# A Perceiver layer on one core: projections in halves, and copies batch by batch

## The chip, the core and the metric

The kernel runs on one core of a Trainium2 chip. The core has five engines with an instruction stream each: PE (matrix products; its weight loads are listed as PEld), DVE (element-wise vector work), ACT (functions and copies with a scale or bias), POOL (general element-wise work) and SP (here it only issues DMA transfers). The engines wait for each other through semaphores. SBUF is the on-chip memory, 128 partitions wide; PE writes its results into the eight banks of PSUM. The metric is the device time of one launch in microseconds, the median of several runs; lower is better.

## The reference

The kernel computes one layer on x of shape 2 x 256 x 512 (two batches of 256 tokens): cross-attention to a context of 2 x 4096 x 256, causal self-attention, and a mixture of experts, each on a normalised input (less its mean, over the root of its variance plus 1e-5) and added to x.

```python
# self-attention, 16 heads of 32 columns:
Q = proj_split(q_w, q_b)
K = proj_split(k_w, k_b)
V = proj_split(v_w, v_b)
S = jnp.einsum('hid,hjd->hij', K, Q) * SCALE
decay = jnp.where(delta < 0, 0.0, -delta.astype(jnp.float32) ** ALPHA)
S = jnp.where(delta < 0, -jnp.inf, S) + decay
C = jax.nn.softmax(S, axis=-1)
attn = jnp.einsum('hij,hjd->hid', C, V)
...
return attn @ o_w.T + o_b
# experts: a gate picks two of 8 per token (not shown), and a shared one:
sh = gelu(xt @ sw1 + sb1) @ sw2 + sb2
sh = sh + gelu(xt @ swd) @ swu
out = out + 0.2 * sh
# the layer:
x = x + _L0_xattn_ref(_layernorm(x, axis=-1), ctx_1024, mask_BxS2_bf1, ...)
x = x + _L0_attn_ref(_layernorm(x, axis=-1), ...)
x = x + _L0_ffn_ref(_layernorm(x, axis=-1), ...)
```

## The kernel before

Four stages follow one another: `queries` (to about 50 us), `cross` (to about 1419), `selfattn` (1420 to 1531) and `experts` (1532 to the end). Many products are made in three parts: an operand is split into a rounded high half (names in `h` or `_hi`, written by ACT) and the rest (`l` or `_lo`, written by DVE), and high x low, low x high and high x high are summed in PSUM. A product over 512 input columns so takes 3 x 4 = 12 matrix instructions of 128 rows each. The order of the work on each engine is the order in which the code is written; nothing reorders it.

**Cross-attention.** A unit is one key-value head of one batch. Its 4096 context tokens come in 8 stretches `n` of 4 steps `q`. At each step ACT copies the turned probabilities (`pth`, L688), DVE makes the rest (`ptl`, L860), and PE multiplies with the values (L1096). In the first part of batch 1 (`first_part(1)`) ACT also makes the high halves of that batch's value weights (`values_weight_high`, L742, twice, at n = 2 and n = 6) and of the output weight (`output_weight_high`, L716, at n = 2), and DVE the rest (`values_weight_low`, L915). All three stand at the head of their stretch, before its step q = 0.

**Self-attention.** `xn`, the normalised input, is turned on PE and split (`xh`, `xl`, L1376). Values for both batches, query 0 and key 0 are projected (`project`, L1447; 12 products of 128 x 512). Then come N = 8 units: unit n is chunk n // 2 of four heads, for batch n % 2. A unit has two turns `it` (query rows of the first and of the second 128 tokens). For a unit: PE makes all scores (L1474, sixteen records), DVE adds the mask and takes the maximum (L1318), ACT the exponential (L1394), DVE the reciprocal of the sum (L1326), POOL the scaling (L1270; of the second turn DVE does half, L1330), PE turns the probabilities (L1492), ACT and DVE copy them (`cT`, L1399, L1343), PE multiplies with the values (L1504), and ACT and DVE store the output's halves (L1403, L1334). The units overlap: in body n PE first issues the scores of unit n + 1, then the first turn of unit n, then the values of unit n - 1, then the second turn of unit n. Queries and keys of the chunks 1 to 3 are made beside the units, as tables say: `QUERY_BESIDE = {0: 1, 1: 2, 3: 3}` and `KEY_BESIDE = {0: 1, 2: 2, 4: 3}`. A query is copied out of PSUM by DVE (`query`, L1292), a key by ACT (`key`, L1380); both use one bank, `made`, so each projection waits until the one before has been copied. The scores of a chunk wait for its query and key.

**Experts' front.** `xn` of the third normalisation is turned on PE batch by batch (L2011). ACT copies the turned input twice, 512 columns (both batches) at a time: rounded (`xTh`, L1904) and whole (`xnT`, L1905); DVE makes the rest `xTl` from PSUM (L1766). ACT's root of the variance of batch 1 (`ln_root`, L107) stands before these copies. PE then makes the gate's logits (L2018, eight records) from `xnT`, and the shared expert's first product (L2027). The rest of the stage, to the end, is PE's work on the shared expert and the eight experts.

`WARM` is a number of priming products of the identity at the head of a stage, before PE's first wait.

## Time and profile before

| | us |
|---|---|
| median of 3 runs | 1980.34 |
| lowest and highest | 1979.60, 1981.26 |
| the profiled execution's own time | 1978.39 |
| its span in the profile | 1976.7 |
| mean granted clock of PE (1 is the full 2.4 GHz) | 0.987 |
| PE busy | 1909.9 (97%) |
| DVE busy | 1095.7 (55%) |
| ACT busy | 979.2 (50%) |
| POOL busy | 328.9 (17%) |

The profiled execution is 1.95 us under the median, and its own time is 1.69 us more than its span. Busy shares are averages over four stages. The lines of a timeline give start, duration, engine, source line, operation, output and inputs, and a count where equal instructions follow one another; in brackets stand the idle time before and what ended it. The durations of such a group include the tail of the last instruction, so starts are compared with starts. The windows split the span into stretches and give each engine's busy time with the count of its instructions.

### The profile page before, as it was taken

To read this page: it belongs to the slowest core of one execution; us is meant where nothing else is said; L and a number is where in the kernel's file an instruction comes from. 1 tells how busy PE (TensorE), PEld (TensorE's weight loads), DVE (VectorE), ACT (ScalarE), POOL (GpSimd) and SP (SyncE) were. 2 spreads that over 40 slices of the span, in tenths; PEclk is the share of its full clock that TensorE was granted. 3 is DMA by queue.
4 is the path that set the end of the run, shared out by engine and by line. 5 is a ranking of instruction groups with operands and counts; after the bars stand their busy time and mean duration, and the time that the engine had idled before them with its cause. 6 is when DMAs were issued, how large, how long until landed. Compare 5 with 4: busy or idle time off the path is not lost. (4 is left out here: it accounts for less than half of the span.)

```text
span 1976.7 us, 32080 instructions
## 1 busy us (share of the span) xinstructions
PE 1909.9 (97%) x10486; PEld 1602.1 (81%) x10486; DVE 1095.7 (55%) x2443; ACT 979.2 (50%) x2075; POOL 328.9 (17%) x238
## 2 busy tenths in 40 slices
PE   9999999999999999999999999999877899999998
PEld 6787888888888778878888888887655688999997
DVE  3667677677667666776677676676645531000002
ACT  3204676576577572065775776676544442122111
POOL 0300211211211213011211212211642300000001
PEclk9999999999999999999999999999988999999999
DMA  8651111111111146501111111111300907577552
GB/s 245 211 195 44 41 43 40 50 32 50 45 32 37 43 155 199 169 25 46 33 51 40 37 45 40 37 43 55 105 1 1 353 18 265 196 269 263 203 187 66
DMA packets 123281, 198.12 MB, mean 100 GB/s; under 512 B 12741, under 2 KB 62021, under 8 KB 119104
## 3 DMA queue, kind: packets, MB, share of 16 engines
q1 hardware_dynamic: 119040, 188.59, 28.6%
q10 hardware_dynamic: 2880, 4.55, 0.7%
q0 software_dynamic: 1280, 3.93, 0.6%
q8 instruction: 47, 0.77, 0.2%
q14 instruction: 34, 0.28, 0.0%
HBM read 151.50 MB, written 45.81 MB: 100 GB/s over the span
## 5 line engine op out<-in xcount | busy, mean ns | idle before, releaser
L860 DVE TENSOR_TENSOR crs_ptl<-crs_tp,crs_pth 128x512 fp32r<-128x512 f32 x512 | 352.7, 690 | 178.9 <-ACT crs_pth L688 178.3
L688 ACT ACTIVATE crs_pth<-crs_tp 128x512 fp32r<-128x512 f32 x504 | 301.6, 599 | 245.1 <-PE crs_tp L1086 241.9
L606 POOL TENSOR_TENSOR crs_vl<-crs_vraw,crs_vh 128x512 fp32r<-128x512 f32 x128 | 164.9, 1288 | 1071.2 <-ACT crs_vh L695 1071.1
L1077 PE MATMUL crs_ring<-crs_kh,crs_ql 128*128 128x512 f32 x512 | 233.9, 457 | 0.3 <-DVE crs_kl L864 0.3
L1096 PE MATMUL crs_ov<-crs_ptl,crs_vh 128*128 128x512 f32 x512 | 209.8, 410 | 9.6 <-DVE crs_ptl L860 7.7
L1096 PE MATMUL crs_ov<-crs_pth,crs_vh 128*128 128x512 f32 x512 | 202.5, 396 | 0.0
L1077 PE MATMUL crs_ring<-crs_kh,crs_qh 128*128 128x512 f32 x512 | 202.2, 395 | 0.0
L1077 PE MATMUL crs_ring<-crs_kl,crs_qh 128*128 128x512 f32 x512 | 201.3, 393 | 0.0
L1096 PE MATMUL crs_ov<-crs_pth,crs_vl 128*128 128x512 f32 x512 | 199.6, 390 | 0.0
L1086 PEld LDWEIGHTS crs_tp<-all_ident,crs_prob 128*128 128x128 f32 x1024 | 143.3, 141 | 69.1 <-ACT crs_more L677 4.2
L1086 PE MATMUL crs_tp<-all_ident,crs_prob 128*128 128x128 f32 x1024 | 195.3, 272 | 3.3 <-ACT crs_more L677 3.3
L677 ACT ACTIVATE crs_prob<-crs_prob,crs_nmax 128x512 f32<-128x512 f32 (+1 forms) x192 | 166.5, 868 | 63.3 <-DVE crs_nmax L875 63.3
L1086 PE MATMUL crs_tp<-all_ident,crs_more 128*128 128x128 f32 x1024 | 195.9, 273 | 0.0
L870 DVE CUSTOM_DVE_ANT_0 crs_more<-crs_ring,crs_maskb 128x512 f32<-128x512 f32 x256 | 172.7, 682 | 0.0
L870 DVE CUSTOM_DVE_ANT_0 crs_prob<-crs_ring,crs_maskb 128x512 f32<-128x512 f32 x256 | 172.5, 682 | 0.2 <-DVE attn_norm_ln_rstd L119 0.2
L677 ACT ACTIVATE crs_more<-crs_more,crs_nmax 128x512 f32<-128x512 f32 (+1 forms) x192 | 166.1, 865 | 0.0
L1878 DVE TENSOR_SCALAR ex_yT<-moe_bank,moe_b_cols 128x160 f32<-128x160 f32 x32 | 10.8, 379 | 273.1 <-PE moe_bank L2150 273.1
L864 DVE TENSOR_TENSOR crs_kl<-crs_ring,crs_kh 128x512 fp32r<-128x512 f32 x128 | 88.4, 691 | 132.0 <-ACT crs_kh L699 132.0
L1965 ACT ACTIVATE ex_hT<-moe_bank,moe_b_cols 128x160 f32<-128x160 f32 x128 | 43.5, 391 | 235.4 <-PE moe_bank L2126 235.4
L2126 PE MATMUL moe_bank<-moe_bufT,moe_w 128*128 128x160 f32 x1024 | 145.2, 302 | 0.7 <-ACT moe_bufT L1960 0.7
L2126 PEld LDWEIGHTS moe_bank<-moe_bufT,moe_w 128*128 128x128 f32 x1024 | 141.3, 192 | 2.8 <-ACT ex_hT L1965 1.0
L1086 PEld LDWEIGHTS crs_tp<-all_ident,crs_more 128*128 128x128 f32 x1024 | 127.9, 141 | 0.0
(283 smaller groups left out, 3344.0 us busy)
## 6 DMA issues: line engine op xcount, KB each, us to landing
moe_w<-in_L_ffn_w SPq DMA_DIRECT2D x48, 1024.0 KB, 12.7
v_scratch<-crs_more SPq DMA_DIRECT2D x64, 512.0 KB, 2.9
crs_vraw<-v_scratch SPq DMA_DIRECT2D x128, 256.0 KB, 2.7
ex_w<-in_L_ffn_w SPq DMA_DIRECT2D x16, 1024.0 KB, 13.9
crs_prob<-in_ctx SPq DMA_DIRECT2D x16, 512.0 KB, 4.7
crs_wo<-in_L_xattn_Wo SPq DMA_DIRECT2D x16, 512.0 KB, 4.2
moe_w<-in_L_ffn_sw SPq DMA_DIRECT2D x8, 1024.0 KB, 13.4
qry_wq<-in_L_xattn_Wq SPq DMA_DIRECT2D x16, 256.0 KB, 3.6
```

Of the source, the lines that this page charges most:

```text
L606: nc.gpsimd.tensor_tensor(vl[:, n % VR, :, :], vraw[:, :, :], vh[:, n % VR, :, :].bitcast(F32), ALU.subtract).then_inc(s["v_lo"], 1)
L677: act.activation(w, w, ACT.Exp, bias=nmax[:, t:t + 1], accum_out=rs[:, t, PIECE_OF[n]:PIECE_OF[n] + 1]).then_inc(s["p_ready"], 1)
L688: act.activation(pth[:, k % PT, :], tp[k % PT][:, :], ACT.Copy).then_inc(s["pt_hi"], 1)
L860: v.tensor_tensor(ptl[:, k % PT, :], tp[k % PT][:, :], pth[:, k % PT, :].bitcast(F32), ALU.subtract).then_inc(s["pt_lo"], 1)
L864: v.tensor_tensor(kl[:, n % KR, :], ring[k_at(n, op) % RING][:, :], kh[:, n % KR, :].bitcast(F32), ALU.subtract).then_inc(s["ring_free"], 1)
L870: v.tensor_tensor_reduce(probs(t, n * BANK, (n + 1) * BANK), ring[at % RING][:, :], maskb[:, n * BANK:(n + 1) * BANK], op0=ALU.add, op1=AL ...
L1077: m = pe.matmul(ring[at % RING][:, :], a[:, t // RT, rows], w[:, n % KR, :], start=i == 0, stop=i == 2)
L1086: m = pe.transpose(tp[k % PT][:, t * P:(t + 1) * P], probs(t, k * P, (k + 1) * P), ident[:, :])
L1096: m = pe.matmul(ov[:, :], a[:, k // NC % VR, k % NC, :], w[:, k % PT, :], start=k == 0 and i == 0, stop=k == SCH - 1 and i == 2)
L1878: m = v.tensor_scalar(yT[:, c, :], y_ps[c // 2][:, c % 2 * SL:(c % 2 + 1) * SL], b_cols[:, bass.ds(e * KC + c, 1)], None, ALU.add)
L1965: m = act.activation(hT[:, 2 * n + q, :], h_ps[n % 2][:, q * SL:(q + 1) * SL], ACT.Gelu, bias=b1_cols[:, bass.ds(e * FC + (2 * n + q), 1)])
L2126: m = pe.matmul(h_ps[n % 2][:, q * SL:(q + 1) * SL], w1[i][:, c, fc * P:(fc + 1) * P], bufT[:, i, c, :], start=c == 0, stop=c == KC - 1)
```

## The change

**A, cross-attention.** In `first_part(1)` the value weights' copies move behind the first step of their stretch, and the output weight's copy behind the third, on ACT; DVE's rest of the value weights moves likewise. Batch 0 keeps its places.

```diff
@@ -750,13 +750,14 @@
                             exp_piece(u, 0, t)
                         exp_piece(u, 1, 0)
                         exp_piece(u, 1, 1)
-                    if n == (2 if b else 0):
-                        values_weight_high(b, 0)
-                    if b and n == 2:
-                        output_weight_high(u, first_base(b) + QT)
-                    if n == (6 if b else 3):
-                        values_weight_high(b, 1)
                     for q in range(NC):
+                        if q == (1 if b else 0):
+                            if n == (2 if b else 0):
+                                values_weight_high(b, 0)
+                            if n == (6 if b else 3):
+                                values_weight_high(b, 1)
+                        if b and n == 2 and q == 3:
+                            output_weight_high(u, first_base(b) + QT)
                         if b and n < SB:
                             pt_high(u, n * NC + q)
                             exp_ahead(u, n, q)
```

On ACT, at the start of stretch n = 2 of batch 1's first part, before (`crs_pth` are the probabilities' copies, `crs_kh` receives the value weights, `crs_woh` the output weight):

```order
L695 ACTIVATE crs_vh<-crs_vraw 128x512 [waits crs_pv_done,crs_v_ld]
L742 ACTIVATE crs_kh<-crs_more 128x1024 [waits crs_ring_full,crs_wv_ld]
L716 ACTIVATE crs_woh<-crs_wo 128x1024 [waits crs_ring_full,crs_wo_ld]
L688 ACTIVATE crs_pth<-crs_tp 128x512 [waits crs_pv_done,crs_pt_full]
L677 ACTIVATE crs_more,crs_rs<-crs_more,crs_nmax 128x1024 [waits crs_inv_chain,crs_max_ready]
L688 ACTIVATE crs_pth<-crs_tp 128x512 [waits crs_pv_done,crs_pt_full]
```

and now:

```order
L695 ACTIVATE crs_vh<-crs_vraw 128x512 [waits crs_pv_done,crs_v_ld]
L688 ACTIVATE crs_pth<-crs_tp 128x512 [waits crs_pv_done,crs_pt_full]
L677 ACTIVATE crs_more,crs_rs<-crs_more,crs_nmax 128x1024 [waits crs_inv_chain,crs_max_ready]
L742 ACTIVATE crs_kh<-crs_more 128x1024 [waits crs_ring_full,crs_wv_ld]
L688 ACTIVATE crs_pth<-crs_tp 128x512 [waits crs_pv_done,crs_pt_full]
L677 ACTIVATE crs_more,crs_rs<-crs_more,crs_nmax 128x1024 [waits crs_inv_chain,crs_max_ready]
L732 ACTIVATE all_w_hi<-crs_prob 128x2x512 [waits crs_ring_full,crs_ctx_ld1]
L688 ACTIVATE crs_pth<-crs_tp 128x512 [waits crs_pv_done,crs_pt_full]
L716 ACTIVATE crs_woh<-crs_wo 128x1024 [waits crs_ring_full,crs_wo_ld]
```

The probabilities' copy of the first step now comes ahead of both weight copies, and a copy of the context (L732) and two probability copies stand between them.

**B, self-attention.** `WARM` becomes 1. Query 1 moves ahead of the first scores, behind key 0. Query 0 is made in two pieces of 160 and 352 columns, in 24 products. The five remaining projections, one per body n = 0 to 4, are made in halves of six products: the first behind the values of the unit before, the second behind the second turn. On DVE the query's copy moves from before the reciprocal of the second turn to behind the next unit's first reciprocal.

```diff
@@ -1182,10 +1184,10 @@
     N = B * KC
     BANKS = RT + 1
 
-    QUERY_BESIDE = {0: 1, 1: 2, 3: 3}
+    QUERY_BESIDE = {1: 2, 3: 3}
     KEY_BESIDE = {0: 1, 2: 2, 4: 3}
 
-    WARM = 2
+    WARM = 1
     with ExitStack() as ctx:
         t = Tensors(nc, ctx, "att")
         xn = t.sb("xn", [P, TT, D])
@@ -1348,12 +1351,12 @@
             for n in range(N):
                 if n < N - 1:
                     scores(n + 1, 0)
-                if n in QUERY_BESIDE:
-                    query(QUERY_BESIDE[n])
                 inverse(n, 1)
                 if n < N - 1:
                     scores(n + 1, 1)
                     inverse(n + 1, 0)
+                if n in QUERY_BESIDE:
+                    query(QUERY_BESIDE[n])
                 turned(n)
                 if n:
                     output_low(n - 1)
@@ -1441,25 +1444,35 @@
                     m = pe.matmul(v_ps[i % 2][:, :], y[:, c, i * P:(i + 1) * P], wt[:, V_W, c, :], start=n == 0, stop=n == 3 * KC - 1)
                 m.then_inc(s["v_ps"], 1)
 
-            def project(w, o, to, done):
-
-                for n, (wt, y, c) in enumerate((wt, y, c) for wt, y in ((w_lo, xh), (w_hi, xh), (w_hi, xl)) for c in range(KC)):
-                    m = pe.matmul(to[:, :], wt[:, w, c, o * P:(o + 1) * P], y[:, c, :], start=n == 0, stop=n == 3 * KC - 1)
-                m.then_inc(done, 1)
-
-            def query(c):
-                if c:
+            def project(w, o, to, done, part):
+
+
+                for cols in ((slice(0, 160), slice(160, B * TQ)) if (w, o) == (Q_W, 0) else (slice(0, B * TQ),)):
+                    for n, (wt, y, c) in enumerate((wt, y, c) for wt, y in ((w_lo, xh), (w_hi, xh), (w_hi, xl)) for c in range(KC)):
+                        if part is None or n // (3 * KC // 2) == part:
+                            m = pe.matmul(to[:, cols], wt[:, w, c, o * P:(o + 1) * P], y[:, c, cols], start=n == 0, stop=n == 3 * KC - 1)
+                if part != 0:
+                    m.then_inc(done, 1)
+
+            def query(c, part=None):
+                if c and part != 1:
                     pe.wait_ge(s["q_ok"], c)
-                if c > 1:
-                    pe.wait_ge(s["k_ok"], c)
-                project(Q_W, c, made, s["q_ps"])
-
-            def key(c):
+                    if c > 1:
+                        pe.wait_ge(s["k_ok"], c)
+                project(Q_W, c, made, s["q_ps"], part)
+
+            def key(c, part=None):
                 if c == 0:
                     pe.wait_ge(s["w_lo"], 2)
-                else:
+                elif part != 1:
                     pe.wait_ge(s["q_ok"], c + 1)
-                project(K_W, c, made if c else o_bank, s["k_ps"])
+                project(K_W, c, made if c else o_bank, s["k_ps"], part)
+
+            def beside(n, part):
+                if n in QUERY_BESIDE:
+                    query(QUERY_BESIDE[n], part)
+                if n in KEY_BESIDE:
+                    key(KEY_BESIDE[n], part)
 
             def scores(n, it):
                 if n and it == 0:
@@ -1537,16 +1551,10 @@
                         scores(n + 1, 0)
                         scores(n + 1, 1)
                     transposes(n, it)
-                    if it == 0:
-                        if n in QUERY_BESIDE:
-                            query(QUERY_BESIDE[n])
-                        elif n in KEY_BESIDE:
-                            key(KEY_BESIDE[n])
-                        if n:
-                            values(n - 1, 0)
-                            values(n - 1, 1)
-                    elif n in QUERY_BESIDE and n in KEY_BESIDE:
-                        key(KEY_BESIDE[n])
+                    if it == 0 and n:
+                        values(n - 1, 0)
+                        values(n - 1, 1)
+                    beside(n, it)
             out(0)
             values(N - 1, 0)
             values(N - 1, 1)
```

On PE in body n = 1, which makes query 2, before (`att_turn` are turned probabilities, `att_made` the bank of the projection, `att_o` the values' products, `att_s` the scores):

```order
L1492 MATMUL att_turn<-all_ident,att_sc 128x128 x3
L1447 MATMUL att_made<-att_xh,all_w_lo 128x512 [waits att_k_ok,att_q_ok]
L1447 MATMUL att_made<-att_xh,all_w_lo 128x512 x3
L1447 MATMUL att_made<-att_xh,all_w_hi 128x512 x4
L1447 MATMUL att_made<-att_xl,all_w_hi 128x512 x4
L1504 MATMUL att_o<-att_cT,att_V 32x128 [waits att_cT_ok]
L1504 MATMUL att_o<-att_cT,att_V 32x128 x3
L1504 MATMUL att_o<-att_cT,att_V 32x128 [waits att_cT2_ok,att_cT_ok]
L1504 MATMUL att_o<-att_cT,att_V 32x128 x7
L1492 MATMUL att_turn<-all_ident,att_sc 128x128 [waits att_cT2_ok,att_norm2_ok,att_norm_ok]
L1492 MATMUL att_turn<-all_ident,att_sc 128x128 x3
```

and now, from the values on to the scores of the unit after next:

```order
L1517 MATMUL att_o<-att_cT,att_V 32x128 x7
L1453 MATMUL att_made<-att_xh,all_w_lo 128x512 [waits att_k_ok,att_q_ok]
L1453 MATMUL att_made<-att_xh,all_w_lo 128x512 x3
L1453 MATMUL att_made<-att_xh,all_w_hi 128x512 x2
L1505 MATMUL att_turn<-all_ident,att_sc 128x128 [waits att_cT2_ok,att_norm2_ok,att_norm_ok]
L1505 MATMUL att_turn<-all_ident,att_sc 128x128 x3
L1505 MATMUL att_turn<-all_ident,att_sc 128x128 [waits att_cT_ok]
L1505 MATMUL att_turn<-all_ident,att_sc 128x128 x3
L1453 MATMUL att_made<-att_xh,all_w_hi 128x512 x2
L1453 MATMUL att_made<-att_xl,all_w_hi 128x512 x4
L1487 MATMUL att_s<-att_qT,att_kT 128x128 [waits att_k_ok,att_q_ok,att_s_ok]
```

The twelve products that stood before the values stand in two sixes on either side of the second turn.

On DVE in the first body that copies a query, before (`att_nmax` is the negated maximum, `att_qT` the query, `att_rsum` the sums):

```order
L1322 TENSOR_SCALAR att_nmax<-att_mx 128x4 [waits att_s_ok]
L1292 TENSOR_SCALAR att_qT<-att_made,att_bias_cols 128x512 [waits att_q_ps]
L1326 RECIPROCAL att_rsum<-att_rsum 128x4 [waits att_exp_ok]
L1330 TENSOR_TENSOR att_sc<-att_sc,att_rsum 128x512 [waits att_inv_ok]
L1318 ISA att_sc,att_mx<-att_s,att_decay 128x256 [waits att_t_ps,att_s_ps]
```

and now in body n = 1:

```order
L1325 TENSOR_SCALAR att_nmax<-att_mx 128x4 [waits att_s_ok]
L1329 RECIPROCAL att_rsum<-att_rsum 128x4 [waits att_exp_ok]
L1294 TENSOR_SCALAR att_qT<-att_made,att_bias_cols 128x512 [waits att_q_ps]
L1346 COPY att_cT<-att_turn 128x512 [waits att_t_ps]
L1337 TENSOR_TENSOR att_ol<-att_o,att_oh 128x256 [waits att_o_hi]
```

The query's copy no longer stands between a unit's maximum and its reciprocal; the copy of the second turn and the output's rest stand behind it.

**C, experts' front.** `WARM` becomes 1. ACT copies the turned input in 256 columns, one batch at a time: for batch 0 both copies of each of the four blocks, then the root, then for batch 1 the rounded copies alone. DVE makes the whole copies of batch 1, and then the rest `xTl` from the copies in SBUF. The gate's products wait for all eight whole copies.

```diff
@@ -1760,10 +1768,14 @@
             ln_deviation(v, ch, norm, RT, TT, s["root_ready"], 1)
             for i in range(RT, TT):
                 ln_scale(v, X, xn, norm, i, s["xn_ready"] if i == TT - 1 else None)
+            second = slice(TQ, B * TQ)
             for c in range(KC):
-
-                v.wait_ge(s["xT_ok"], c + 1)
-                v.tensor_tensor(xTl[:, c, :], bank[c][:, :], xTh[:, c, :].bitcast(F32), ALU.subtract).then_inc(s["xT_lo"], 1)
+                v.wait_ge(s["xT_ps"], KC + c + 1)
+                v.wait_ge(s["xT_hi"], KC + c + 1)
+                v.tensor_copy(xnT[:, c, second], bank[c][:, second]).then_inc(s["xT_ok"], 1)
+            v.wait_ge(s["xT_ok"], B * KC)
+            for c in range(KC):
+                v.tensor_tensor(xTl[:, c, :], xnT[:, c, :], xTh[:, c, :].bitcast(F32), ALU.subtract).then_inc(s["xT_lo"], 1)
             v.wait_ge(s["rows_ld"], 64)
 
             def first_low(n, q):
@@ -1897,12 +1909,16 @@
             act.dma_start(b_cols[:, 0:SB1], a["L0_ffn_b2"]).then_inc(r, 16)
             act.dma_start(b_cols[:, SB1:SB1 + FC], a["L0_ffn_sb1"]).then_inc(r, 16)
             act.dma_start(sb2[:, :], a["L0_ffn_sb2"].rearrange("(o d) -> o d", o=1).to_broadcast([P, D])).then_inc(r, 16)
-            act.wait_ge(s["var_ready"], 1)
-            ln_root(act, norm, RT, TT, s["root_ready"])
-            for c in range(KC):
-                act.wait_ge(s["xT_ps"], c + 1)
-                act.activation(xTh[:, c, :], bank[c][:, :], ACT.Copy)
-                act.activation(xnT[:, c, :], bank[c][:, :], ACT.Copy).then_inc(s["xT_ok"], 1)
+            for b in range(B):
+                for c in range(KC):
+                    w = slice(b * TQ, (b + 1) * TQ)
+                    act.wait_ge(s["xT_ps"], b * KC + c + 1)
+                    if b == 0:
+                        act.activation(xnT[:, c, w], bank[c][:, w], ACT.Copy).then_inc(s["xT_ok"], 1)
+                    act.activation(xTh[:, c, w], bank[c][:, w], ACT.Copy).then_inc(s["xT_hi"], 1)
+                if b == 0:
+                    act.wait_ge(s["var_ready"], 1)
+                    ln_root(act, norm, RT, TT, s["root_ready"])
 
             def first_high(n, q, early):
                 if not early:
@@ -2008,11 +2024,13 @@
                 pe.wait_ge(s["xn_ready"], b + 1)
                 for c in range(KC):
                     for i in range(b * RT, (b + 1) * RT):
+                        if b and i == RT:
+
+                            pe.wait_ge(s["xT_hi"], c + 1)
                         m = pe.transpose(bank[c][:, i * P:(i + 1) * P], xn[:, i, c * P:(c + 1) * P], ident[:, :])
-                    if b == B - 1:
-                        m.then_inc(s["xT_ps"], 1)
-
-            pe.wait_ge(s["xT_ok"], KC)
+                    m.then_inc(s["xT_ps"], 1)
+
+            pe.wait_ge(s["xT_ok"], B * KC)
             pe.wait_ge(s["gate_ld"], 16)
             for c in range(KC):
                 m = pe.matmul(bank[6][0:E, :], gate[:, c, :], xnT[:, c, :], start=c == 0, stop=c == KC - 1)
```

On ACT, before:

```order
L1899 DMA moe_sb<-in_L_ffn_sb 128x512
L107 ACTIVATE ffn_norm_ln_root<-ffn_norm_ln_veps 128x2 [waits moe_var_ready]
L1904 ACTIVATE sh_xTh<-moe_bank 128x512 [waits moe_xT_ps]
L1905 ACTIVATE sh_xnT<-moe_bank 128x512
L1904 ACTIVATE sh_xTh<-moe_bank 128x512 [waits moe_xT_ps]
```

and now, from the copies of the third block of batch 0:

```order
L1917 ACTIVATE sh_xnT<-moe_bank 128x256 [waits moe_xT_ps]
L1918 ACTIVATE sh_xTh<-moe_bank 128x256
L1917 ACTIVATE sh_xnT<-moe_bank 128x256 [waits moe_xT_ps]
L1918 ACTIVATE sh_xTh<-moe_bank 128x256
L107 ACTIVATE ffn_norm_ln_root<-ffn_norm_ln_veps 128x2 [waits moe_var_ready]
L1918 ACTIVATE sh_xTh<-moe_bank 128x256 [waits moe_xT_ps] x4
```

Eight copies stand ahead of the root that was first, and four behind it where there were eight twice as wide.

## Rows read from the trace of the kernel before

**Rows 1.** Page, section 1: busy time of each engine, share of the span.

```profile
PE 1909.9 (97%) x10486; PEld 1602.1 (81%) x10486; DVE 1095.7 (55%) x2443; ACT 979.2 (50%) x2075; POOL 328.9 (17%) x238
```

**Rows 2.** Windows, all engines (PE, PEld, DVE, ACT, POOL), then clock and DMA.

```profile
1500.00:1520.00 20.00, 14.38 (x129) 10.70 (x128) 10.60 (x48) 11.46 (x41) 6.72 (x5) 0.68 0.00 1
```

**Rows 3.** Waits of PE, 1420 to 1570 us: total, times, longest.

```profile
PE att_turn L1492 <- POOL att_sc L1270: 8.3, 5, 2.6
```

**Rows 4.** Timeline of PE: first score products of units; a projection; output's first.

```profile
1442.94 0.94 PE L1474 MATMUL att_s<-att_qT,att_kT 32*128 32x128 f32 x16 [0.93 <-ACT att_kT L1380]
...
1446.96 1.67 PE L1474 MATMUL att_s<-att_qT,att_kT 32*128 32x128 f32 x16 [3.09 <-issue]
...
1449.33 2.06 PE L1447 MATMUL att_made<-att_xh,all_w_lo 128*128 128x512 f32 x4
...
1462.38 0.94 PE L1474 MATMUL att_s<-att_qT,att_kT 32*128 32x128 f32 x16 [0.87 <-ACT att_kT L1380]
...
1480.58 0.94 PE L1474 MATMUL att_s<-att_qT,att_kT 32*128 32x128 f32 x16 [2.66 <-ACT att_kT L1380]
...
1498.61 0.94 PE L1474 MATMUL att_s<-att_qT,att_kT 32*128 32x128 f32 x16 [2.66 <-ACT att_kT L1380]
...
1504.46 1.67 PE L1474 MATMUL att_s<-att_qT,att_kT 32*128 32x128 f32 x16
...
1516.96 2.07 PE L1514 MATMUL att_s<-all_w_hi,att_ol 128*128 128x512 f32 x4 [1.11 <-DVE att_ol L1334]
```

**Rows 5.** Timeline, the unit without a projection, after its score products at 1498.61.

```profile
1500.84 0.40 ACT L1394 ACTIVATE att_sc<-att_sc,att_nmax 128x128 f32<-128x128 f32 x1 [2.37 <-DVE att_nmax L1322]
...
1500.96 1.54 POOL L1270 TENSOR_TENSOR att_sc<-att_sc,att_rsum 128x512 f32<-128x512 f32 x1 [6.73 <-DVE att_rsum L1326]
...
1502.56 1.97 PE L1492 MATMUL att_turn<-all_ident,att_sc 128*128 128x128 f32 x8 [1.04 <-POOL att_sc L1270]
```

**Rows 6.** Timeline of DVE: a query's copy, a second turn's copy.

```profile
1453.80 0.75 DVE L1292 TENSOR_SCALAR att_qT<-att_made,att_bias_cols 128x512 f32<-128x512 f32 x1 [3.92 <-PE att_made L1447]
...
1488.53 0.69 DVE L1343 COPY att_cT<-att_turn 128x512 f32<-128x512 f32 x1 [0.43 <-PE att_turn L1492]
```

**Rows 7.** Timeline of ACT, unit 3: its first exponential, the output copy in between.

```profile
1473.90 0.40 ACT L1394 ACTIVATE att_sc<-att_sc,att_nmax 128x128 f32<-128x128 f32 x1 [1.48 <-DVE att_nmax L1322]
...
1477.04 0.39 ACT L1403 ACTIVATE att_oh<-att_o 128x256 fp32r<-128x256 f32 x1 [1.00 <-PE att_o L1504]
```

**Rows 8.** Timeline of PE, first query and key; page, section 5, 160 columns.

```profile
1436.40 1.07 PE L1447 MATMUL att_made<-att_xh,all_w_lo 128*128 128x512 f32 x4
...
1439.12 1.07 PE L1447 MATMUL att_o<-att_xh,all_w_lo 128*128 128x512 f32 x4
...
L2126 PE MATMUL moe_bank<-moe_bufT,moe_w 128*128 128x160 f32 x1024 | 145.2, 302 | 0.7 <-ACT moe_bufT L1960 0.7
```

**Rows 9.** Timeline, batch 1's first part: ACT and the PE wait behind it.

```profile
705.96 1.05 ACT L716 ACTIVATE crs_woh<-crs_wo 128x1024 fp32r<-128x1024 f32 x1
...
708.27 0.79 PE L1096 MATMUL crs_ov<-crs_ptl,crs_vh 128*128 128x512 f32 x1 [2.43 <-DVE crs_ptl L860]
```

**Rows 10.** Timeline, four 256-column copies of ACT; then the experts' front.

```profile
1422.27 1.21 ACT L1376 ACTIVATE att_xh<-att_s 128x256 fp32r<-128x256 f32 x4 [0.75 <-PE att_s L1430]
...
1533.61 0.52 ACTq L1899 DMA_DIRECT2D moe_sb<-in_L_ffn_sb  x1
...
1534.84 0.20 ACT L107 ACTIVATE ffn_norm_ln_root<-ffn_norm_ln_veps 128x2 f32<-128x2 f32 x1 [2.54 <-DVE ffn_norm_ln_veps L102]
...
1537.13 1.45 PE L2011 MATMUL moe_bank<-all_ident,sh_xn 128*128 128x128 f32 x8 [2.18 <-DVE sh_xn L124]
...
1541.68 5.01 PE L2018 MATMUL moe_bank<-sh_xnT,moe_gate 128*8 128x512 f32 x8 [3.10 <-ACT sh_xnT L1905]
...
1544.44 4.56 POOL L1733 TENSOR_TENSOR all_X<-all_X,moe_sb 128x2048 f32<-128x2048 f32 x1
...
1547.34 2.21 DVE L1771 TENSOR_TENSOR sh_s1l<-moe_w,sh_s1h 128x512 fp32r<-128x512 f32 x1
```

15 lines of the change are left out of this document (9 added, 6 removed).

## The prediction

> **What bounds the kernel now.** I read the page's busy times first: TensorE is busy 97% of the span, 1909.9 of 1976.7 us [rows 1], so a gain must come from the 67 us in which it stands still, or from stretches in which its clock is low. The windows come next: the self-attention is where both happen. Between 1500 and 1520 us PE is busy 14.38 of 20 us, and the granted clock is 0.68 [rows 2], which is a mixture of the two levels, 1.2 and 2.4 GHz. The waits of that stretch say for whom: POOL's scaling of the probabilities alone accounts for 8.3 us in five waits [rows 3]. Last comes the timeline. One unit's score products take 0.94 us at the high level and 1.67 at the low one [rows 4], and the first score products of units 0, 1, 2, 4, 6 and 7 start at 1442.94, 1446.96, 1462.38, 1480.58, 1498.61 and 1504.46, the output projection at 1516.96 [rows 4]. So the intervals are 4.02, 15.42, 18.20, 18.03, 5.85 and 12.50: 74.02 us. The long ones are those that hold projections. Inside them PE stands at a key's copy (2.66 us before units 4 and 6 [rows 4]), and it comes to that copy late because the twelve products of a projection stand before the work that waits for POOL, not in that wait.
>
> **Part B, the self-attention's order.** I rebuild the intervals from the same rows.
>
> *A unit that carries no key (bodies 1 and 3).* From the score products, the second turn of the previous unit can start 3.95 us later, because its probabilities pass DVE's reciprocal and POOL's 1.54 us (1498.61 to 1502.56) [rows 4, 5]. In that unit scores, first turn and values filled PE for 3.95 less the wait of 1.04 [rows 5], 2.9 us at a clock that was partly low; by 0.94 against 1.67 they are 1.6 at the high level throughout, and I take 2.1. A whole projection lasts 1439.12 - 1436.40 = 2.72 us [rows 8], a half 1.36; 2.1 and 1.36 are 3.5 us, so the first half lies in the POOL wait for nothing. Behind it come the second turn, 1.90 us at the low level (1502.56 to 1504.46) [rows 4, 5], about 0.95 at the high one, and the second half, 1.36: 6.3 us.
>
> *A unit that carries a key (bodies 2 and 4).* Here ACT's chain is the longer one. With DVE free, the first exponential comes 2.2 us after the score products (1498.61 to 1500.84) [rows 4, 5]. From unit 3's first exponential to unit 4's score products are 1480.58 - 1473.90 = 6.68 us, of which ACT waited 1.00 before the output's copy for PE's values [rows 4, 7]; the values come earlier now, so 5.7. The query's copy on DVE, 0.75 [rows 6], is moved behind the next unit's first reciprocal, where the turned copy (0.69 [rows 6]) and the next masks queue behind it; I let DVE come 0.8 late. Sum 8.7.
>
> *Unit 0 to 2's interval.* Before, it held a query and a key in full, and a DVE that stood 3.92 us before the query's copy while the reciprocal waited behind it [rows 6]. Now: scores and first turn at the low level 2.37 (1446.96 to 1449.33) [rows 4], half a key at the low level 2.6 (four such products take 2.06 with their tail, against 1.07 at the high one [rows 4, 8]), the second turn 1.4 (between 0.95 and 1.90), the other half 1.36, and from the last product to the next scores 1.1 (1442.94 - 1439.12 - 2.72) [rows 4, 8]: 8.8.
>
> *The rest.* Units 0 to 1 stay 4.0, units 6 to 7 lose the low-level part of the turn, 5.85 - 0.95 = 4.9, and the end, 12.5, has no projection and is kept. The sum is 4.0 + 8.8 + 2 x (6.3 + 8.7) + 4.9 + 12.5 = 60.2, a gain of 13.8.
>
> *What the front gives back.* Query 1 is computed before the first scores: 2.72 more, of which 1.1 lay in the wait for the key's copy: the scores start 1.6 later. Query 0 is split into 160 and 352 columns, 24 products for 12. The 352 columns cost 352/512 x 0.227 = 0.156 each. For 160 columns of this number format no row exists. The one row of that width is the experts', in plain fp32, where each product leaves two records, 1024 records in 145.2 us [rows 8], so 0.284 a product; if width alone counted it would be 0.071. The split thus costs 12 x (0.284 + 0.156 - 0.227) = 2.6 at one end and nothing at the other (with one record a product, 0.85). I take 2.6, the only row of the width, and keep 0 for the range. A second priming product left out of the front is hidden behind the normalised input's arrival. Together +4.2, so part B is worth 13.8 - 4.2 = 9.6. Bounds: 17 if no unit falls to the low clock, the end shrinks too and the split is free; 3 if a third of the units stays at the low clock and DVE's delay doubles.
>
> The Trainium skill's page "TensorE: Matmul & The Clock Gate", section "Back-to-back issue gap", gives for a single product N/2.4 + 2.5 ns. By it (my estimate from the page) 160 and 352 columns cost 69 and 149 ns, and the split would cost about nothing; the sum of part B would be 12.2. The row of 512 agrees (0.227 against 0.216), the one of 160, in the other format, does not.
>
> **Part A, the cross-attention's copies.** In batch 1's first part ACT makes the key buffer's copy and then the output weight's, 1.05 us each, ahead of the next probabilities' copy, and PE waits 2.43 us at 708.27 for it and what DVE makes of it [rows 9]. Two probability copies are now made between them. The first wait shrinks by about 1.9, but the ACT work before the fourth value step is the same; the wait comes back in two pieces before the next steps, and the fourth starts about where it did. What is left is that PE stands less long at a time. I take -0.9; bounds -2.4 (the whole wait) and +0.5 (the pieces are longer than the one).
>
> **Part C, the experts' front.** ACT issues its last transfer until 1534.13 (1533.61 + 0.52) and takes the root for batch 1 at 1534.84 [rows 10]. Now eight copies of 256 columns stand before that root, 0.30 each (four in 1.21) [rows 10]: to 1536.6, so the root and all behind it, DVE's scaling and PE's transposes of batch 1 (1537.13 [rows 10]), come 1.8 later, at 1538.9. Behind them ACT has four copies of 256 instead of eight of 512, and DVE four more; by the same 0.30 to 0.7 each the gate's products can start at 1541.1 to 1541.5 against 1541.68 [rows 10]: a gain of 0.2 to 0.6. But PE stands 1.8 us longer in a row before them, and the gate's eight products, 5.01 us [rows 10] against 8 x 2 x 0.227 = 3.6 at the high clock, may run more of their length at the low level: +0.9. DVE's four subtractions read both inputs from SBUF now, next to POOL's additions: +0.3. Together +0.8; bounds -1.5 (the gate at the high clock) and +6 (next rival but one).
>
> **Sum against the profiled time.** 1978.39 - 0.9 - 9.6 + 0.8 = 1968.7. The median is 1980.34, 1.95 above the profiled execution, so the same program would be timed at 1970.7. The likeliest case's own range is 1966 to 1975.
>
> **Rivals.**
> - *More than forecast.* The split costs nothing (-2.6), the experts' root is not late (-1.7), a further 1 us comes from the end: 1965. For it: width alone may count in a product. Against: the row of 160 columns.
> - *The units stay half at the low clock.* The projections filled long stretches of PE, their halves fill shorter ones. At the low level all through, a unit without a key takes 2.9 + 2.6 + 1.9 + 2.6 = 10.0, one with a key 11.1 (with the copy's 1.1), the first interval 2.37 + 2.6 + 1.9 + 2.6 + 1.1 = 10.6, units 6 to 7 the 5.85 measured: 4.0 + 10.6 + 2 x (10.0 + 11.1) + 5.85 + 12.5 = 75.2. Half of that way is 67.7, a gain of 6.3, and with +4.2, -0.9 and +0.8 the time is 1978.1: no change.
> - *All units at the low clock: slower.* 75.2 is 1.2 above today's 74.02; with 4.2 - 0.9 + 0.8 the time is 1985.6. It decides when about two thirds of the units' work are low: (74.0 - 4.1 - 60.2) / (75.2 - 60.2). For it: clock 0.68 in the unit without a projection [rows 2], and second halves that stand in PE's order ahead of the next scores, so nothing overtakes them. Against: what makes PE wait there is shortened.
> - *DVE's subtractions in contention at the experts' front.* In this stage one DVE subtraction with two SBUF inputs took 2.21 us beside POOL's addition of 4.56, where a turned copy of the same size takes 0.69 [rows 6, 10]. Four subtractions at 2.21 cost 4 x 1.5 = 6.0 where PE waits for them, less what the gate's products hide: part C +5, 1975. The Trainium skill's page "VectorE: DVE Perf Modes", section "Two Vector instructions with no wait between them", says that a second SBUF input is read through an interface shared with GpSimd; the row at 1547.34 agrees. Against: POOL's addition starts at 1544.44 [rows 10], after the subtractions should be done.
>
> **How the numbers follow.** The forecast 0.70, more 0.10, contention 0.08, half low 0.07, all low 0.05. A measurement tells about 0.2% from no change, 4 us. Faster holds the first three and none of the others, less a little for the forecast's upper tail: 0.87; within it 0.08; slower 0.05. Range 1963 to 1977: it takes in the split at nothing, the better case and most of the contention, and leaves out the clock rivals and the far ends.
>
> **What would show it.** Right: query 0's first twelve products near 0.28 us each and the first scores near 1447; the intervals 8.8, 15.0, 15.0 between units 1, 2, 4 and 6; the waits on POOL well under 8.3 us; the experts' root some 2.5 us after ACT's last transfer (before 0.7), and batch 1's transposes 1.8 later in the stage. Wrong: a granted clock under 0.7 through units 1 to 6, halves of a projection longer than 2 us, DVE subtractions over 1 us at the experts' front, or a second turn that still waits over 1 us for POOL.

## The result and the profile after

The changed kernel takes 1968.37 us in the median of five runs (1966.98 to 1972.48), the kernel before 1980.34 (1979.57 to 1981.26): a ratio of 0.9943, 95% interval 0.9928 to 0.9957. The forecast was 1970.7, with a range of 1963 to 1977. The profiled execution has a span of 1966.6 us against 1976.7, 10.1 less.

PE's waits from 1420 to 1560 us, after (total, times, longest):

```profile
PE moe_bank L2030 <- DVE sh_xn L124: 4.4, 1, 4.4
PE att_s L1487 <- ACT att_kT L1383: 4.3, 3, 1.4
...
PE moe_bank L2045 <- DVE sh_s1l L1783: 3.1, 1, 3.1
...
PE att_turn L1505 <- POOL att_sc L1272: 2.7, 5, 1.6
```

The wait for POOL's scaling falls from 8.3 us [rows 3] to 2.7, still five times. The experts' front has a longer single wait than any in this stretch before, 4.4 us for the second batch's normalised input, and a new one of 3.1 for a weight's rest, `s1l`. The timeline of PE through the self-attention, after, answers to [rows 4] and [rows 8]:

```profile
1437.09 0.57 PE L1453 MATMUL att_made<-att_xh,all_w_lo 128*128 128x160 f32 x4
...
1438.39 0.84 PE L1453 MATMUL att_made<-att_xh,all_w_lo 128*128 128x352 f32 x4
...
1440.34 1.08 PE L1453 MATMUL att_o<-att_xh,all_w_lo 128*128 128x512 f32 x4
...
1445.88 0.94 PE L1487 MATMUL att_s<-att_qT,att_kT 32*128 32x128 f32 x16
...
1449.68 1.66 PE L1487 MATMUL att_s<-att_qT,att_kT 32*128 32x128 f32 x16 [2.86 <-issue]
...
1458.30 0.94 PE L1487 MATMUL att_s<-att_qT,att_kT 32*128 32x128 f32 x16 [1.43 <-ACT att_kT L1383]
...
1464.69 0.94 PE L1487 MATMUL att_s<-att_qT,att_kT 32*128 32x128 f32 x16
...
1473.23 0.94 PE L1487 MATMUL att_s<-att_qT,att_kT 32*128 32x128 f32 x16 [1.43 <-ACT att_kT L1383]
...
1479.61 0.94 PE L1487 MATMUL att_s<-att_qT,att_kT 32*128 32x128 f32 x16
...
1488.14 0.94 PE L1487 MATMUL att_s<-att_qT,att_kT 32*128 32x128 f32 x16 [1.43 <-ACT att_kT L1383]
...
1493.13 0.94 PE L1487 MATMUL att_s<-att_qT,att_kT 32*128 32x128 f32 x16
...
1505.58 1.20 PE L1527 MATMUL att_s<-all_w_hi,att_ol 128*128 128x512 f32 x4 [1.11 <-DVE att_ol L1337]
```

The starts give the intervals: 3.80, 8.62, 6.39, 8.54, 6.38, 8.53 and 4.99 us from one unit's scores to the next one's, and 12.45 from unit 7's to the output's first product. Query 0 lasts 1440.34 - 1437.09 = 3.25 us. The ten microseconds are a sum of six stretches, each a difference of starts in the two traces:

| stretch | before | after | difference |
|---|---|---|---|
| to the first value product of the self-attention | 1423.53 | 1424.18 | +0.65 |
| from there to unit 0's scores | 19.41 | 21.70 | +2.29 |
| unit 0's scores to the output's first product | 74.02 | 59.70 | -14.32 |
| output's products, first to last group | 13.02 | 11.36 | -1.66 |
| from there to the shared expert's first product | 16.64 | 19.60 | +2.96 |
| rest of the span | 430.08 | 430.06 | -0.02 |

The experts' front, after, on four engines (start, duration; the count stands at the end):

```profile
1523.27 0.27 ACT L107 ACTIVATE ffn_norm_ln_root<-ffn_norm_ln_veps 128x2 f32<-128x2 f32 x1
...
1525.62 1.97 PE L2030 MATMUL moe_bank<-all_ident,sh_xn 128*128 128x128 f32 x8 [4.39 <-DVE sh_xn L124]
...
1528.57 7.22 DVE L1778 TENSOR_TENSOR sh_xTl<-sh_xnT,sh_xTh 128x512 fp32r<-128x512 f32 x4
1528.59 4.89 PE L2036 MATMUL moe_bank<-sh_xnT,moe_gate 128*8 128x512 f32 x8 [1.00 <-DVE sh_xnT L1775]
...
1530.71 4.53 POOL L1741 TENSOR_TENSOR all_X<-all_X,moe_sb 128x2048 f32<-128x2048 f32 x1
...
1535.72 0.68 DVE L1783 TENSOR_TENSOR sh_s1l<-moe_w,sh_s1h 128x512 fp32r<-128x512 f32 x1
...
1536.54 1.16 PE L2045 MATMUL moe_bank<-sh_xTh,sh_s1l 128*128 128x512 f32 x4 [3.06 <-DVE sh_s1l L1783]
```

and the answer on the tile `sh_xTl` (duration in ns, least, median, largest):

```profile
L1778 DVE TENSOR_TENSOR sh_xTl<-sh_xnT,sh_xTh x4: 679/894/4990, 1528.6 to 1530.8; 128x512 fp32r<-128x512 f32 x4
```

One of DVE's four subtractions lasted 4.99 us. It began when POOL's addition began, and DVE went on half a microsecond after that addition ended at 1535.24. PE had finished the gate and stood 3.06 us. The gate itself starts as far behind the last output product as before (11.65 us against 11.70 [rows 10]) and takes as long, so this wait is the whole of the +2.96.

### The profile page after: what moved, and what is told of

It reads as the page before. It is cut to its first block and busy times, and to the rows that moved or that the text cites. A ratio compares the mean times of both kernels' runs of the same rounds, so it can differ in the third digit from the quotient of the medians.

```text
span 1966.6 us, 32109 instructions
## 1 busy us (share of the span) xinstructions
PE 1904.0 (97%) x10494; PEld 1596.6 (81%) x10494; DVE 1099.3 (56%) x2447; ACT 978.7 (50%) x2079; POOL 327.6 (17%) x238
```

## The experiments

Distances and intervals below are differences of starts in each kernel's own trace. "C" is the distance from the last group of output products to the shared expert's first product.

**Part C: who holds DVE.** Three kernels are the changed one with one edit each, and one has all of part C undone.

```diff
-                v.tensor_tensor(xTl[:, c, :], xnT[:, c, :], xTh[:, c, :].bitcast(F32), ALU.subtract).then_inc(s["xT_lo"], 1)
+                v.tensor_tensor(xTl[:, c, :], bank[c][:, :], xTh[:, c, :].bitcast(F32), ALU.subtract).then_inc(s["xT_lo"], 1)
```

> The changed kernel with one line undone: the rest xTl is subtracted from PSUM again, not from the SBUF copy. In the changed kernel the last of the four subtractions took 4.99 us and ended when POOL's addition ended, and PE's first product of the shared expert stood 19.60 us behind the last output product (16.64 in the kernel before). Theory 1, a DVE instruction with two SBUF inputs is held until POOL's addition is over: the four take about 0.69 each now, but the next instruction, the weight's rest s1l, has two SBUF inputs as well and starts about 0.5 us after POOL's addition began, so it is the one that takes about 4.5 us; the distance stays 19.6 (+-0.3) and the time with it. Theory 2, subtractions from SBUF copies are slow by themselves, or slow under the weights' transfers: the distance falls by about 3, to 16.6, and the time by 3.

Measured: 1966.57 us, ratio to the kernel before 0.9931 (0.9905 to 0.9957); C 1517.37 to 1534.06 = 16.69.

```profile
1529.00 2.48 DVE L1778 TENSOR_TENSOR sh_xTl<-moe_bank,sh_xTh 128x512 fp32r<-128x512 f32 x4
...
1531.40 0.68 DVE L1783 TENSOR_TENSOR sh_s1l<-moe_w,sh_s1h 128x512 fp32r<-128x512 f32 x1
1531.40 5.10 POOL L1741 TENSOR_TENSOR all_X<-all_X,moe_sb 128x2048 f32<-128x2048 f32 x1
...
1534.17 0.68 DVE L1799 COPY moe_rows<-moe_bank 8x512 f32<-8x512 f32 x1 [2.08 <-PE moe_bank L2036]
1534.78 2.28 DVE L1783 TENSOR_TENSOR sh_s1l<-moe_w,sh_s1h 128x512 fp32r<-128x512 f32 x1
...
1534.06 1.19 PE L2045 MATMUL moe_bank<-sh_xTh,sh_s1l 128*128 128x512 f32 x4
```

By the time and by C alone theory 2 would have it; theory 1 had C stay at 19.6, and that part of it missed. The rows say otherwise: the first `s1l` began together with POOL's addition and was through in 0.68, by luck of the start (here it was POOL that took longer, 5.10 us instead of 4.53); the second one, same shape, began in the middle of the addition and took 2.28, ending 0.56 after POOL did. So the hold went to the next instruction with two SBUF inputs that began in the addition, as theory 1 says, but to one for which PE does not wait. DVE's copy from PSUM just before it took 0.68 in the middle of the addition. The four subtractions from PSUM lie ahead of the addition, so this run does not show whether they would be held by it.

```diff
             pool.wait_ge(c, 8)
+            pool.wait_ge(s["s2_lo"], 1)
             nc.gpsimd.tensor_tensor(X[:, :, :], X[:, :, :], sb2[:, :]...
```

> The changed kernel, with POOL's addition of the shared bias to X waiting until the first second-layer rest (s2l) of the shared expert is made; nothing else. Theory 1 (held by POOL's addition): the four subtractions take 0.69 each, so do s1l and s2l; PE's first product follows the gate's, the distance from the last output product falls from 19.60 to about 16.6, time -3.0 us. POOL's 4.5 us lie beside small DVE work after that; one of these may be held up to 4.5 us, hidden by the shared expert. Theory 2 (slow by themselves or by transfers): the subtractions stay at 1.8 on average, no gain.

Measured: 1969.55 us, ratio 0.9942 (0.9922 to 0.9962); C 16.75.

```profile
1531.73 2.91 DVE L1779 TENSOR_TENSOR sh_xTl<-sh_xnT,sh_xTh 128x512 fp32r<-128x512 f32 x4
...
1536.85 1.20 PE L2046 MATMUL moe_bank<-sh_xTh,sh_s1l 128*128 128x512 f32 x4
...
1538.99 4.58 POOL L1742 TENSOR_TENSOR all_X<-all_X,moe_sb 128x2048 f32<-128x2048 f32 x1 [4.60 <-DVE sh_s2l L1788]
...
1540.77 2.86 DVE L1808 TENSOR_TENSOR moe_lg<-moe_lg,moe_small 128x32 f32<-128x32 f32 x1
```

With nothing but POOL's addition moved, the same four subtractions from SBUF take 2.91 us instead of 7.22, and the hold falls on a small instruction of the routing on `moe_lg` with two SBUF inputs: 2.86 us, ending 0.06 behind the addition, where the same instruction took 0.19 in the kernel with `xTl` from PSUM. That settles the cause: theory 1. C falls by 2.85 as expected, but the time does not. The shared expert's third group of products starts 14.80 us behind the first, against 12.60 in the changed kernel: the addition now stands beside the routing, and the rest of the span is 430.95. That the routing's delay costs PE this time is likely and was not tested.

```diff
-            nc.gpsimd.tensor_tensor(X[:, :, :], X[:, :, :], sb2[:, :].unsqueeze(1).to_broadcast([P, TT, D]), ALU.add).then_inc(c, 1)
+            for i in range(TT):
+                m = nc.gpsimd.tensor_tensor(X[:, i, :], X[:, i, :], sb2[:, :], ALU.add)
+            m.then_inc(c, 1)
```

> The changed kernel with POOL's addition cut into four of 128x512 (same elements). Theory 1 with the hold lasting for one POOL instruction: no DVE instruction takes over about 1.8 us (0.7 and one quarter of POOL's 4.5); the distance falls from 19.60 to 17.0 to 18.0, time -2 us. Theory 1b, DVE is held for the whole series: the 4.99 us instruction and the 19.6 stay. Theory 2: the subtractions stay at 1.8 on average.

Measured: 1969.05 us, ratio 0.9948 (0.9929 to 0.9967); C 17.43.

```profile
1528.40 3.98 DVE L1780 TENSOR_TENSOR sh_xTl<-sh_xnT,sh_xTh 128x512 fp32r<-128x512 f32 x4
...
1530.54 6.36 POOL L1742 TENSOR_TENSOR all_X<-all_X,moe_sb 128x512 f32<-128x512 f32 x4
...
1532.31 1.75 DVE L1785 TENSOR_TENSOR sh_s1l<-moe_w,sh_s1h 128x512 fp32r<-128x512 f32 x1
```

The hold lasts for one POOL instruction: with four short ones no DVE instruction of this front takes over 1.8 us, C is inside the range expected, and POOL in its turn takes 6.36 instead of 4.53. The rest of the span grew to 431.8, so the time did not fall by what C did; why was not looked into.

Part C undone (the experts' stage of the kernel before):

> The changed kernel with part C undone: the experts' stage as before the change. By the two traces part C cost 2.96 us (19.60 against 16.64 from the last output product to the shared expert's first product): time about 3.0 below the changed kernel, 1965.4 against 1968.4. By the forecast's sum of part C (+0.8) only 0.8 below; if the SBUF hold was an accident of that one execution, no difference.

Measured: 1965.22 us, ratio 0.9926 (0.9903 to 0.9950). The time is as expected from the traces, but its own execution has C at 18.21, not 16.64: the gate's eight products took longer.

```profile
1524.74 6.57 PE L2026 MATMUL moe_bank<-sh_xnT,moe_gate 128*8 128x512 f32 x8 [2.86 <-ACT sh_xnT L1913]
```

In the execution of before these took 5.01 [rows 10]. The granted clock in the gate's products is 0.54 here and was 0.71 there, so 1.6 us of C can come and go with the clock. The ratios' intervals of the four kernels and of the changed one overlap; what is shown of part C is shown by the traces. `WARM` was not varied by itself, here or in part B.

**Part B: what the order gives.** First the place of the five projections, made whole.

```diff
-                    beside(n, it)
+                    if it == 0:
+                        beside(n, None)
```

> The changed kernel with the five projections beside the units made whole again, all twelve products behind the values and before the second turn, everything else as changed (query 1 ahead, the query's copy late on DVE). Theory 1 (the halves are what gives the gain, because the second turn must not wait): the second turn comes 1.4 later in each body, what hangs on it as well, and the intervals from unit 0's scores to the output's first product, 59.7 in the changed kernel, grow by 3 to 5 us. Theory 2 (PE's own work and ACT's chain set the intervals; the gain is from the order behind the values and the query's copy moved): a unit without a key is 0.86 + 0.42 + 0.8 + 2.72 + 0.95 = 5.8 instead of 6.4, one with a key stays 8.5, the first about 8 to 9; sum 58 to 59, time -1.

The same with `it == 1`, behind the second turn:

> The changed kernel with the five projections made whole behind the second turn. PE then stands until POOL's scaling is done (3.95 us behind the scores), and the whole projection follows: without a key 3.95 + 0.95 + 2.72 = 7.6 against 6.4, with a key 7.6 and 1.1 for the copy = 8.7 against 8.5, the first interval 9.5 against 8.6; sum 63.4 against 59.7, time +3.7. If the gain has nothing to do with where the products stand relative to POOL's wait, the sum stays at 59.7.

Then the two orders apart. With PE's as before the change (the projection whole ahead of the values) and DVE's as changed:

```diff
-                    if it == 0 and n:
+                    if it == 0:
+                        beside(n, None)
+                    if it == 0 and n:
                         values(n - 1, 0)
                         values(n - 1, 1)
-                    beside(n, it)
```

> The changed kernel with the five projections whole and back in their old place on PE, ahead of the values; DVE's copy of a query stays late, behind the next unit's first reciprocal. The four intervals from unit 2's to unit 6's scores are 36.2 us before the change, 29.8 in the changed kernel and 29.5 with whole projections behind the values. Theory 1 (what held the units was DVE's query copy ahead of the reciprocal): about 30 here. Theory 2 (what held them was the projection ahead of the values): about 34 to 36 here.

and with PE's as in the first of these kernels, and DVE's query copy where it was:

```diff
                     scores(n + 1, 0)
+                if n in QUERY_BESIDE:
+                    query(QUERY_BESIDE[n])
                 inverse(n, 1)
...
-                if n in QUERY_BESIDE:
-                    query(QUERY_BESIDE[n])
```

> The changed kernel with the five projections whole behind the values, and DVE's copy of a query back in its old place, ahead of the reciprocal of the second turn. Theory 1 (DVE's query copy held the units): the reciprocal waits for the query, whose twelve products end about 4.8 us behind the scores; with the copy 0.75, the reciprocal and POOL's 1.54 the second turn comes at about 7.7, and the bodies with a query take 8.6 instead of 6.9 on average: the four intervals sum to 33 to 34. Theory 2 (the place of the projection on PE): about 30.

Measured, intervals between the scores of units 2 to 6 (bodies 1 and 3 carry a query, 2 and 4 a key):

| projections on PE | DVE's query copy | query bodies | key bodies | sum | time, ratio (interval) |
|---|---|---|---|---|---|
| whole, ahead of the values (before) | early | 8.54, 7.84 | 9.66, 10.19 | 36.2 | 1980.34 |
| whole, ahead of the values | late | 6.01, 6.02 | 10.00, 10.00 | 32.0 | 1973.34, 0.9967 (0.9956 to 0.9979) |
| whole, behind the values | early | 9.72, 8.86 | 8.48, 8.49 | 35.6 | 1975.27, 0.9979 (0.9970 to 0.9989) |
| whole, behind the values | late | 7.62, 6.09 | 7.91, 7.92 | 29.5 | 1968.20, 0.9938 (0.9921 to 0.9955) |
| halves (changed) | late | 6.39, 6.38 | 8.54, 8.53 | 29.8 | 1968.37, 0.9943 (0.9928 to 0.9957) |
| whole, behind the second turn | late | 9.36, 7.77 | 10.90, 9.30 | 37.3 | 1976.10, 0.9981 (0.9970 to 0.9993) |

Halving gives nothing: 29.5 and 29.8, and the sums from unit 0's scores to the output are 59.55 and 59.70. Of the two theories put against each other for the first of these kernels the second comes near (58 to 59) and the first does not (62.7 to 64.7). Body by body, three of the four are even shorter with whole projections, by 0.3 and twice 0.6; the fourth, 7.62, ran with a granted clock of 0.78, its twin of 6.09 with 1.00. So the equal sums hide a loss by the halves and a low clock in that one execution; whether the low clock belongs to the order is open.

The two moves do different things. The query's copy on DVE decides the bodies with a query. Before the change, DVE and PE in body 3:

```profile
1484.88 0.75 DVE L1292 TENSOR_SCALAR att_qT<-att_made,att_bias_cols 128x512 f32<-128x512 f32 x1 [2.12 <-PE att_made L1447]
...
1487.40 1.09 PE L1492 MATMUL att_turn<-all_ident,att_sc 128*128 128x128 f32 x8 [1.76 <-POOL att_sc L1270]
```

In the kernel with the copy early and the projections behind the values, in body 1:

```profile
1460.65 0.75 DVE L1294 TENSOR_SCALAR att_qT<-att_made,att_bias_cols 128x512 f32<-128x512 f32 x1 [3.11 <-PE att_made L1453]
1461.32 0.17 DVE L1329 RECIPROCAL att_rsum<-att_rsum 128x4 f32<-128x4 f32 x1
...
1463.17 1.97 PE L1505 MATMUL att_turn<-all_ident,att_sc 128*128 128x128 f32 x8 [2.56 <-POOL att_sc L1272]
```

DVE stands 3.11 us for the query while the reciprocal waits behind it, and PE then stands 2.56 for POOL. With the copy late, in the changed kernel and with whole projections ahead of or behind the values, PE does not wait for POOL in these bodies. The place of the projection decides the bodies with a key. With it ahead of the values, ACT and PE in body 2:

```profile
1470.02 0.39 ACT L1406 ACTIVATE att_oh<-att_o 128x256 fp32r<-128x256 f32 x1 [2.07 <-PE att_o L1517]
...
1473.56 0.94 PE L1487 MATMUL att_s<-att_qT,att_kT 32*128 32x128 f32 x16 [2.66 <-ACT att_kT L1383]
```

ACT stands 2.07 us for the values before it can go on to the key's copy, for which PE stands 2.66. In the changed kernel ACT works without a pause from unit 3's first exponential to the key's copy:

```profile
1467.56 0.40 ACT L1397 ACTIVATE att_sc<-att_sc,att_nmax 128x128 f32<-128x128 f32 x1 [2.09 <-DVE att_nmax L1325]
```

From there to unit 4's scores are 5.67 us; the exponential itself comes 2.87 behind unit 3's scores. With whole projections behind the values these are 5.66 and 2.25: the halves cost the key bodies 0.6 because in the changed kernel DVE copies the query 0.11 us behind the scores, not 0.77 ahead of them, and comes later to the next maximum. The expectations of both kernels had one mechanism for all four bodies, and both sums, 32.0 and 35.6, lie between or outside what either theory gave. Behind the second turn the sum from unit 0 to the output is 67.58, +7.9 and not the +3.7 expected, because in bodies 0 to 2 the projection runs at the low clock behind the wait for POOL. In body 1:

```profile
1462.43 1.83 PE L1505 MATMUL att_turn<-all_ident,att_sc 128*128 128x128 f32 x8 [1.63 <-POOL att_sc L1272]
1463.91 2.06 PE L1453 MATMUL att_made<-att_xh,all_w_lo 128*128 128x512 f32 x4
```

Bodies 3 and 4, at a granted clock of 1.00 (0.78 in bodies 0 to 2), take 7.77 and 9.30 against the 7.6 and 8.7 expected. With nothing ahead of the second turn PE waits 1.63 for POOL: that is the wait which products put there fill.

Query 1 back beside unit 0, the other bodies as changed:

```diff
-    QUERY_BESIDE = {1: 2, 3: 3}
+    QUERY_BESIDE = {0: 1, 1: 2, 3: 3}
...
-            query(1)
...
-                    beside(n, it)
+                    if n:
+                        beside(n, it)
+                    elif it == 0:
+                        query(1)
+                    else:
+                        key(1)
```

> The changed kernel with query 1 back beside unit 0: query 1 whole behind the first turn of unit 0, copied by DVE before the reciprocal of the second turn, key 1 whole behind that turn, as before the change; bodies 1 to 4 in halves as changed. The first scores come 1.7 earlier (1440.34 + 3.82 = 1444.2 against 1445.88, counted from the same start), and the interval from unit 1's to unit 2's scores is the 15.4 us of before instead of 8.6: time +5.1. If it was the halves in bodies 1 to 4 alone that gave the gain, the interval stays below 10 and the time is 1.7 lower.

Measured: 1971.38 us, ratio 0.9965 (0.9953 to 0.9978). Unit 0's scores come 19.97 us behind the first value product instead of 21.70 (-1.73), and the interval from unit 1 to 2 is

```profile
1446.86 1.67 PE L1488 MATMUL att_s<-att_qT,att_kT 32*128 32x128 f32 x16 [2.83 <-issue]
...
1462.13 0.94 PE L1488 MATMUL att_s<-att_qT,att_kT 32*128 32x128 f32 x16 [0.87 <-ACT att_kT L1384]
```

15.27, against 8.62. Both intervals are as expected: the new order around unit 0 gives 6.6 us for 1.7 in front of it; the four bodies give 6.4. In unit 0's body query 1, the halves of key 1 and DVE's copy were put back together, and their shares are not told apart. The time rose by 3.0 and not by 5.1. In the profiled execution, whose span is 2.3 us longer, the self-attention began 1.06 us earlier than in the changed kernel's, and the end, from unit 7's scores to the output, took 10.90 instead of 12.45.

**Part A undone:**

```diff
-                        if q == (1 if b else 0):
-                            if n == (2 if b else 0):
-                                values_weight_high(b, 0)
...
+                    if n == (2 if b else 0):
+                        values_weight_high(b, 0)
```

> The changed kernel with part A undone: the weight copies of batch 1's first part stand at the head of their stretch again. By the two traces the wait at 708 us is spread, and the last value product of the cross-attention comes 0.86 us earlier with part A (1414.04 before, 1413.17 after), but in the changed kernel's execution PE's clock was at the low level in the products right behind it, so that the self-attention began 0.65 later all the same. Theory 1 (part A is worth its 0.9, the low clock there is chance): the last value product at 1414.0 +-0.2, time 0.9 above the changed kernel, not to be told from it. Theory 2 (part A brings the low clock with it): the last value product at 1414.0, the clock there at the high level, and the self-attention begins 0.6 earlier than in the changed kernel.

Measured: 1969.92 us, ratio 0.9955 (0.9938 to 0.9971). The last value product of the cross-attention starts at 1413.78; in twelve executions with part A it starts between 1412.06 and 1414.12, 1413.2 in the mean. The self-attention's first value product starts at 1423.50; with part A between 1421.48 and 1424.91, mean 1423.2. Theory 2 does not hold: the products behind the last value product run at the high level without part A and in eight of the twelve executions with it (9.4 to 9.8 us from the last value product to the self-attention's first one; 11.0 in the other four, the changed kernel's among them).

The traces show what part A does. In all twelve executions with it the wait of 2.43 us at 708 [rows 9] has become two; in the changed kernel:

```profile
707.52 0.47 PE L1098 MATMUL crs_ov<-crs_ptl,crs_vh 128*128 128x512 f32 x1 [0.81 <-POOL crs_vl L606]
...
710.50 0.50 PE L1098 MATMUL crs_ov<-crs_ptl,crs_vh 128*128 128x512 f32 x1 [1.61 <-DVE crs_ptl L861]
```

Together they are 2.42: PE does not wait less. What differs is the clock behind them. Counted from PE's wait of 0.55 us at about 699, the granted clock from 9 to 20 us later is 0.84 to 0.85 in both executions without part A and in four of the twelve with it, and 1.00 in the other eight. In these eight PE comes to its next long wait for ACT, at about 864, 163.9 to 164.3 us behind the same start, in the six others 165.3 to 165.6. The mean with part A is 0.9 lower, but two executions without it are too few to tell this from chance, and the times do not tell it either. Part A stays undecided.

**A better version.** The changed kernel with query 0 whole, `xTl` from PSUM, and ACT's root ahead of all copies, or behind those of two blocks:

```diff
-                for cols in ((slice(0, 160), slice(160, B * TQ)) if (w, o) == (Q_W, 0) else (slice(0, B * TQ),)):
+                for cols in (slice(0, B * TQ),):
...
+                    if b == 0 and c == 0:    # 2 in the second kernel
+                        act.wait_ge(s["var_ready"], 1)
+                        ln_root(act, norm, RT, TT, s["root_ready"])
                     act.wait_ge(s["xT_ps"], b * KC + c + 1)
```

> The changed kernel with three mends: query 0 whole in 512 columns (12 products), xTl subtracted from PSUM, and ACT's root ahead of all copies at the experts' front. Query 0: -0.53 by the changed kernel's trace (3.25 against 2.72 us). xTl from PSUM: -2.9 as measured. Root: it waits for the variance at 1.8 us into ACT's copies instead of standing behind 3.2 us of them, so the normalised second batch and PE's turns of it come about 1.4 earlier, and the gate's products with them: -1.4, if the weight's rest still comes before POOL's addition. Distance from the last output product to the shared expert's first: 15.2 to 15.5. Time about 4.8 below the changed kernel, 1963.5. If the clock at the gate or POOL's addition decides instead, the distance stays at 16.7 and the time at 1965.

> As the one before, but ACT's root behind the copies of two of the four blocks of batch 0, about when the variance is ready: the root comes about 0.4 later than with the root first and ACT does not stand idle for it. Distance 15.5 to 15.8 if the root's time decides; equal to or below the other if ACT's copies decide. Time 1963.5 to 1964.

Measured: 1964.77 us, ratio 0.9934 (0.9918 to 0.9949), C 15.58; and 1964.05 us, 0.9922 (0.9910 to 0.9934), C 16.01. From the first value product to unit 0's scores it is 0.52 and 0.55 less than in the changed kernel, and PE's wait for the second batch's input falls from 4.39 us to 2.86 and 3.29. In the second kernel:

```profile
1527.88 2.48 DVE L1778 TENSOR_TENSOR sh_xTl<-moe_bank,sh_xTh 128x512 fp32r<-128x512 f32 x4
1527.90 5.63 PE L2036 MATMUL moe_bank<-sh_xnT,moe_gate 128*8 128x512 f32 x8 [1.00 <-DVE sh_xnT L1775]
...
1533.46 1.19 PE L2045 MATMUL moe_bank<-sh_xTh,sh_s1l 128*128 128x512 f32 x4
```

The gate's products now end last there: 5.92 and 5.63 us at granted clocks of 0.60 and 0.63. They start 1.9 and 1.2 us earlier than in the changed kernel, so the root's time decides their start, as expected, but they take longer, and both distances lie just above their ranges (15.2 to 15.5 and 15.5 to 15.8). Against the kernel before the second is faster by 0.8% (0.7 to 0.9); against the changed kernel the two stand about 4 us lower in the median, but the intervals of their ratios overlap. Part C left out altogether, 0.9926 above, does as well: that the mended part C is worth keeping is suggested by the distance (15.58 and 16.01 against 16.64) and not shown by the time.

## Why the prediction came out

**The intervals, right.** Forecast 4.0, 8.8, 6.3 and 8.7 twice, 4.9, 12.5, sum 60.2; measured 3.80, 8.62, 6.39, 8.54, 6.38, 8.53, 4.99, 12.45, sum 59.70. The key bodies were worked out from ACT's chain with its 1.00 us wait for the values gone, and the runs with the projections moved show that this is what ends them: forecast 2.2 + 0.8 + 5.7, measured 2.87 + 5.67. The clock rivals did not come: the score products of units 2 to 7 are all 0.94, and the granted clock from 1449 to 1494 us is 0.96.

**The reason given for the query bodies, not what made them shorter.** "The first half lies in the POOL wait for nothing" is true as far as it goes: in these bodies the second turn no longer waits for POOL, and it waits 1.63 where the projection stands behind it. But before the change a whole projection stood ahead of that turn too, and PE still waited 1.76; and whole projections with the query's copy late give bodies as short (6.0 to 6.1 at the full clock). Those bodies got shorter because DVE's reciprocal no longer stands behind the query's copy. The prediction saw that hold (3.92 us) only in the first interval; in the others it took for granted that it is gone, with a second turn 3.95 us behind the scores. The number came out since that turn was read from a unit without a query copy.

**The front, mis-sized.** Forecast +4.2, measured +2.29. The 1.6 for query 1 is 1.73. The split of query 0 costs 3.25 - 2.72 = 0.53 and not 2.6: a product of 160 columns takes (1438.39 - 1437.09)/12 = 0.108 us. The term leaned on the only row of that width, in plain fp32, and the two formats do not compare. The better rival, which had the split at nothing, was nearer on this term.

The Trainium skill's page "TensorE: Matmul & The Clock Gate", section "Back-to-back issue gap", would have had, by an estimate from its N/2.4 + 2.5 ns, 0.069 and 0.149 us for 160 and 352 columns; measured are 0.108 and 0.162. For 160 columns it is nearer than the row that was used, and for both it is under the measured cost.

**The experts' front, mis-sized by a rival's mechanism.** Forecast +0.8, measured +2.96. The root is late as forecast: PE's wait before the second batch's turns rose from 2.18 to 4.39, 2.2 against the 1.8 of the sum. The shorter copies behind it make up for that: the gate starts 0.05 earlier, where the sum had 0.2 to 0.6, and its products take as long as before, where the sum had +0.9. The term that failed is the DVE subtractions, put at +0.3: PE stands 3.06 for what lies behind them, because DVE is held by POOL's addition, the rival at 0.08. That rival's price was put as four subtractions of 2.21 each; it was one of 4.99. The reason against it, that the addition starts too late, was wrong by the move of the subtractions: they begin 9.5 us into the stage (6.6 before), and POOL's addition at 11.6 (12.3 before), since its wait for the bias' transfer is over earlier.

The Trainium skill's page "VectorE: DVE Perf Modes", section "Two Vector instructions with no wait between them", says that DVE's second SBUF input is read through an interface shared with GpSimd. The runs agree: four subtractions with two SBUF inputs took 7.22 us with the addition beside them and 2.91 without it.

**Part A and the clock, by chance.** Forecast -0.9, and the last value product did come 0.87 earlier in that execution; then eight products behind it ran at the low clock, and the stretch ended at +0.65. What the forecast named as left of the change, that PE stands less long at a time, the traces show; that it is worth 0.9 they do not. The output's products, not in the sum, gained 1.66 by the clock. Forecast and measured sums, -9.7 and -10.1, agree more closely than their terms: the front (-1.9), the intervals (-0.5) and the output (-1.7) came out better, part A (+1.6) and the experts' front (+2.2) worse.

**The signs.** Of the signs of being wrong two came: a DVE subtraction of 4.99 us at the experts' front, and a second turn that waits 1.63 for POOL (1.04 before [rows 5]), but only in unit 6's body, which has no projection. Of the signs of being right one failed: query 0's first twelve products are 0.108 us each, not 0.28.

## What to carry over

Before an order on one engine is changed, look which engine's queue holds the instruction that everything waits for: here a copy that nothing needed soon stood ahead of a reciprocal, and on ACT a key's copy behind an output's. Moving these, and query 1 ahead of the units, gave the gain; cutting the projections in halves gave none. When a copy is redirected from PSUM to SBUF, look what POOL does in that stretch: a DVE instruction with two SBUF inputs may be held until POOL's instruction is over.

## What the runs showed of the hardware

A DVE subtraction of 128x512 with both inputs in SBUF took 0.68 us alone and 2.28 and 4.99 us when it began in the course of a POOL addition of 128x2048; it ended 0.5 to 0.6 us after POOL's instruction. With additions of 128x512 the longest of this front was 1.78. With one input in PSUM no hold was seen: in the cross-attention of the kernel before, such a subtraction took its usual time inside a POOL subtraction with two SBUF inputs.

```profile
1331.64 2.40 POOL L610 TENSOR_TENSOR crs_wol<-crs_wo,crs_woh 128x1024 fp32r<-128x1024 f32 x1
...
1332.09 0.68 DVE L860 TENSOR_TENSOR crs_ptl<-crs_tp,crs_pth 128x512 fp32r<-128x512 f32 x1
```

It seems to go the other way round too. POOL's scaling of 128x512 in the self-attention takes 1.04 us in a unit's first turn; in the second turn, where DVE's own half of the scaling (two SBUF inputs, 0.69) starts 0.04 to 0.05 earlier, it takes 1.54 to 1.55, in every unit before and after. No run separates this from the other shape of the second turn. The 1.54 that the forecast took from [rows 5] as POOL's time is the longer one.

Executions of nearly the same code differ by the clock in stretches with waits. From unit 7's scores to the last group of output products the changed kernel took 12.45 + 11.36 us; with part C undone, which does not touch that stretch, 10.90 + 11.35; and with `xTl` from PSUM, which does not either, 12.88 + 13.16. The windows of 1495 to 1520 us (PE busy, then the granted clock), first with part C undone:

```profile
1495.00:1520.00 25.00, 18.60 (x128) 1.00 0.15 43
```

then with `xTl` from PSUM:

```profile
1495.00:1520.00 25.00, 20.35 (x121) 0.80 0.00 1
```

The first ran at the full clock throughout, the second in part at the low level. These 4 us are as much as the mends of the better version are worth, so a single execution's time does not tell them; the stretches do.
